# ScalarE issues the store of a tile's normed rows and the load of a later x tile, in place of SyncE

## The chip, the cores and the metric

The kernel runs on one core of a Trainium2 chip. The metric is the device time of one execution in microseconds (us). Five engines work side by side, each through its own list of instructions, in order: TensorE (PE in the profile), VectorE (DVE), ScalarE (ACT), GpSimd (POOL) and SyncE (SP), which here only issues DMAs. They meet at semaphores: an instruction can wait until a semaphore has reached a value, and can raise one when it is done.

## What is computed

The program is one layer of a Perceiver-like network on `x` (64 batches of 32 rows, 512 wide) with a context of 257 rows per batch. Cut to what matters:

```python
x = x + xattn(layernorm(x), ctx)      # 16 heads, keys = values = context, then @ W_out.T + b_out
x = x + attn(layernorm(x), ...)       # low-rank q, k, v with a rotation, 16 heads, then @ Wo + bo
x = x + ffn(layernorm(x), ...)        # 8 experts, each row to the one of its largest gate
```

The third normalisation is what the change is near. Its result is stored to a scratch tensor in DRAM, tile by tile, because the expert stage at the end gathers rows from it in another order, expert by expert:

```python
logits = xf @ Wg + bg                 # xf = layernorm(x) after the second attention
idx = argmax(softmax(logits))
out = (gelu(xf @ W1[idx] + b1[idx]) @ W2[idx] + b2[idx])
```

## The kernel before

The 2048 rows of `x` are 16 tiles of 128 rows (`T = 16`), each of four batches (`BT = 4`). Time is laid out by hand in steps: a batch has 11 steps (`STEPS`), a tile 44 (`TILE`), and every engine's program runs over the same steps and emits at each step the pieces of work that are due there. Tables of numbers (`SCALE3 = 105`, `X2 = 100`, `NORM_HI = 20` and so on) say how many steps after the start of a tile's successor a stage stands; a second table (`LATER`) shifts the last two tiles. So three tiles are in work at once: while batch b of tile t + 3 goes through the cross attention (scores, softmax, turned probabilities, product with the context), tile t + 2 goes through the dense products of the self attention (query, key and value columns, L571 to L573), and tile t is finished: its residual sum x2 is made (DVE), stored (SP, L546), measured (DVE), its root is taken (POOL), and ACT normalises it into the one buffer `norm3` (L905, from the stage `SCALE3`; the profile calls the buffer `norm`).

At that place ACT's list has, in this order: `norm_w`, the second normalisation of tile t + 2 (L905, stage `SCALE1`); `norm`, the third one of tile t (L905, `SCALE3`); `operand_hi`, the high part of tile t + 2's normed and transposed rows (L966, `NORM_HI`); then the exponentials of the next batch (L943). `operand_hi` is what DVE needs to make `operand_lo` (L1147), and PE needs both for the 48 dense products of the tile (L571 to L573), which start with a wait for `operand_lo`.

The x tiles lie in four buffers, `x_tile[t % 4]`. A buffer is free when x2 of its tile has been stored (`x2_stored`) and the third normalisation has read it (`normed_r`); then the x rows of four tiles on are loaded into it (`load_x`, L478). DVE measures them (`stats_x`, L1060, six steps later) for the first normalisation. SP's list is: the key loads of each batch (L470, four DMAs of 128 KB), the context load (L463), and in one batch of each tile the store of x2 (L546), the load of x (L478) and the store of `norm3` (L550). SP waits in order too, so what stands behind a wait waits with it.

The expert stage comes last: slots of 128 rows, gathered with indirect DMAs from both scratch tensors, with PE as the busiest engine.

Of the kernel before, what the change touches and what calls it, by code (L numbers as in the profile page):

```python
# [10 lines left out]
P = 128  # L11
# [5 lines left out]
T = B * S // P  # L17
# [30 lines left out]
SCALE3, CHOOSE, RANK, RANKED = 105, 103, 105, 106  # L48
# [130 lines left out]
def tile_at(step, offset, later=(0, 0)):  # L179

    for t in (T - 2, T - 1):
        if step == TILE * (t + 1) + offset + later[t - T + 2]:
            return t
    t, rest = divmod(step - offset, TILE)
    return t - 1 if rest == 0 and 1 <= t <= T - 2 else -1
# [15 lines left out]
def program(nc, ins, out, const_at, x2_dram, norm3_dram):  # L201
# [50 lines left out]
    x_tile = [sba(f"x_tile{i}", [P, D]) for i in range(2)] + [x_pair[:, i, :] for i in range(2)]  # L252
    norm_x, norm_w, norm3 = (sba(n, [P, D]) for n in ("norm_x", "norm_w", "norm3"))
# [98 lines left out]
    x_loaded = [signal(f"x_loaded{i}") for i in range(4)]  # L352
# [6 lines left out]
    x2_stored = [signal(f"x2_stored{i}") for i in range(4)]  # L359
    norm3_stored = signal("norm3_stored")  # L360
# [26 lines left out]
    measured_r, rstd_r, normed_r = signal("measured_r"), signal("rstd_r"), signal("normed_r")  # L387
# [66 lines left out]
    x_rows = ins["x"].rearrange("b s d -> (b s) d").rearrange("(t p) d -> t p d", p=P)  # L454


    def sync_program():
        sp, until = nc.sync, Until(nc.sync)

        def load_context(b):  # L460
            until.wait_ge(attended, 2 * (b - 4) + 2)
            src = ins["ctx_1024"][b, 0:C2 * P, :].rearrange("(p c) d -> p c d", c=C2)
            sp.dma_start(context[b % 4][:, :, :], src).then_inc(context_loaded[b % 4], 16)  # L463

        def load_keys(b):
            until.wait_ge(keys_turned, 2 * (b - 2) + 2)
            for hl in range(HL):
                src = ins["ctx_1024"][b, 0:C2 * P, hl * G * HD:(hl + 1) * G * HD].rearrange("(n j c) d -> j c n d", j=HD, c=C2)
                dst = keys[b % 2][hl * HD:(hl + 1) * HD, :, :, :, :].rearrange("p c n g d -> p c n (g d)")
                sp.dma_start(dst, src).then_inc(keys_loaded[b % 2], 16)  # L470

        def load_x(t):
            if t >= 2:
                until.wait_ge(unit_done, UNITS.index(("rot", 0)) + 1)
            if t >= 4:
                until.wait_ge(x2_stored[t % 4], 16 * (t // 4))
                until.wait_ge(normed_r, t - 3)
            sp.dma_start(x_tile[t % 4][:, :], x_rows[t]).then_inc(x_loaded[t % 4], 16)  # L478

        def load_weight(dst, name, loaded):  # L480
            sp.dma_start(dst, ins[name].rearrange("(k p) n -> p k n", p=P)).then_inc(loaded, 16)

        def broadcast(dst, name):
            src = ins[name]
            sp.dma_start(dst, src.unsqueeze(0).broadcast_to([P, src.shape[0]])).then_inc(small_loaded, 16)

        def load_small():
            broadcast(bias_xout[:, :], "L0_xattn_b_out")
            broadcast(bias_g[:, :], "L0_ffn_bg")
            sp.dma_start(out_bias[:, :], ins["L0_attn_Wo_b"].rearrange("(g p) -> p g", p=P),  # L490
                          allow_slow_non_contiguous=True).then_inc(small_loaded, 16)
            sp.dma_start(wg[:, :, :], ins["L0_ffn_Wg"].rearrange("(g p) e -> p g e", p=P)).then_inc(small_loaded, 16)
            broadcast(bias_qk[:, 0, :], "L0_attn_Wq_r_b")
            broadcast(row_uq[:, :], "L0_attn_Wu_q_b")
            broadcast(bias_qk[:, 1, :], "L0_attn_Wk_r_b")
            broadcast(row_uk[:, :], "L0_attn_Wu_k_b")
            broadcast(bias_v[:, 0:D], "L0_attn_Wu_v_b")
            broadcast(bias_out[:, :], "L0_attn_Wo_b")

        load_x(0)  # L500
        sp.dma_start(consts[:, :], ins["const"][:, 0:kept_columns]).then_inc(const_loaded, 16)
        load_keys(0)
        sp.dma_start(last_rows[0:B, :], ins["ctx_1024"][:, J - 1, :]).then_inc(last_loaded, 16)
        load_weight(staged_b[:, :, 0:DQ], "L0_attn_Wd_q_w", staged_b_loaded)
        load_weight(staged_b[:, :, DQ:2 * DQ], "L0_attn_Wd_kv_w", staged_b_loaded)
        load_keys(1)
        load_context(0)
        load_weight(staged_c[:, 2:4, :], "L0_attn_Wq_r_w", staged_c_loaded)
        load_weight(staged_c[:, 0:2, :], "L0_attn_Wu_q_w", staged_c_loaded)
        load_context(1)  # L510
        load_weight(staged_a[:, :, :], "L0_xattn_W_out", staged_a_loaded)
        load_keys(2)
        load_weight(staged_d[:, :, :], "L0_attn_Wk_r_w", staged_d_loaded)
        load_context(2)
        load_context(3)
        a, b = const_at["rope"]
        sp.dma_start(consts_1[:, :], ins["const"][:, a:b]).then_inc(tables_loaded, 16)
        a, b = const_at["before"][0], const_at["all"][1]
        sp.dma_start(tables[:, 0:b - a], ins["const"][:, a:b]).then_inc(tables_loaded, 16)

        for step in range(LAST_STEP):
            b, k = divmod(step, STEPS)
            t, bl = divmod(b, BT)
            if k == 5 and bl == 1 and t + 1 < T:
                load_x(t + 1)
            if k == 2 and 1 <= b and b + 3 < B:
                load_context(b + 3)
            if k == KEYS_LOAD_AT and 1 <= b and b + 2 < B:
                load_keys(b + 2)
            if step == UNIT_AT[4]:  # L530
                until.wait_ge(unit_done, 4)
                load_weight(staged_b[:, 0:2, :], "L0_attn_Wu_k_w", staged_b_loaded)
                load_weight(staged_b[:, 2:4, :], "L0_attn_Wu_v_w", staged_b_loaded)
            if step == BIAS_LOAD_AT:
                load_small()
            if step == UNIT_AT[13]:
                until.wait_ge(unit_done, 13)
                load_weight(staged_a[:, :, :], "L0_attn_Wo_w", staged_a_loaded)
            if step >= TILE and step % 2 == 0 and step < TILE + 2 * E:
                e = (step - TILE) // 2  # L540
                sp.dma_start(b1_all[:, E - 1 - e, :], ins["L0_ffn_b1"][e].rearrange("(k p) -> p k", p=P),
                             allow_slow_non_contiguous=True).then_inc(b1_loaded, 16)
            t = tile_at(step, X2, LATER["X2"])
            if t >= 0:
                until.wait_ge(x2_made, t + 1)
                sp.dma_start(x2_dram[t * P:(t + 1) * P, :], x_tile[t % 4][:, :]).then_inc(x2_stored[t % 4], 16)  # L546
            t = tile_at(step, SCALE3, LATER["SCALE3"])
            if t >= 0:
                until.wait_ge(normed_r, t + 1)
                sp.dma_start(norm3_dram[t * P:(t + 1) * P, :], norm3[:, :]).then_inc(norm3_stored, 16)  # L550
            if step == STEPS * (B + 1):
                until.wait_ge(attended, 2 * B)
                until.wait_ge(plast_kept, 2 * B)
                until.wait_ge(scored, 2 * B)
                until.wait_ge(k_last_moved, 2 * B)
                for e in range(EARLY):
                    load_expert(sp, e)
# [334 lines left out]
    def scalar_program():  # L892
        act, until = nc.scalar, Until(nc.scalar)
# [10 lines left out]
        def scale(x, dst, n, done):  # L904
            act.activation(dst, x, ACT.Identity, bias=shift[n][:, :], scale=rstd[n][:, :]).then_inc(done, 1)  # L905
# [40 lines left out]
        def stages(step):  # L946
            t = tile_at(step, QUERIES_MOVE)
            if t >= 1:
                place_queries(t)
            t = tile_at(step, ATT_HI, LATER["ATT_HI"])  # L950
# [4 lines left out]
            t = tile_at(step, SCALE1, LATER["SCALE1"])  # L955
# [6 lines left out]
            t = tile_at(step, NORM_HI, LATER["NORM_HI"])  # L962
# [4 lines left out]
            t = tile_at(step, Q_MOVE, LATER["Q_MOVE"])  # L967
# [32 lines left out]
            if t >= 0:  # L1000
                until.wait_ge(rstd_r, t + 1)
                until.wait_ge(norm3_stored, 16 * t)
                if t == 0:
                    until.wait_ge(bias_made, 1)
                scale(x_tile[t % 4][:, :], norm3[:, :], "r", normed_r)
            if step == PLACE_RANKS:
                until.wait_ge(in_row_made, 1)
                act.activation(row_in_row[:, 0:T - 2, :], in_row[:, 0:T - 2, :], ACT.Copy, scale=const("row")).then_inc(own_rows_made, 1)
# [11 lines left out]
        for step in range(LAST_STEP):  # L1020
# [16 lines left out]
            t = b // BT  # L1037
# [893 lines left out]
```

## Time and profile before

| what | value |
|---|---|
| three runs | 768.64, 772.24, 772.39 us; median 772.24 |
| profiled execution | 773.6 us, of which the span from first to last instruction is 771.8 |
| granted TensorE clock, mean | 0.989 |
| busy: PE, PE weight loads, DVE, ACT, POOL | 703.2, 547.1, 582.1, 430.8, 335.2 us |
| DMA, mean over the span | 167 GB/s; SP's queue 49.9% of 16 engines' span, ACT's queue 0.0% |
| one tile in the steady part | 30.7 to 32.8 us |

The busy times say which engine is nearest to its limit, over stages that differ. How much an edit costs is read from the waits at its place: an instruction that stands behind an idle stretch is released by the engine named in brackets, and only delays that reach PE's list move the end. Rows of engines are what the engine executes; rows with a "q" (SPq, ACTq) are the issue of a DMA by that engine's sequencer.

### The profile page before, as it was taken

How to read it: one execution, taken by the hardware profiler on the slowest of the kernel's cores; microseconds unless marked ns; L12 is line 12 of the kernel's file. 1: busy time of each engine (PE TensorE's matmuls, PEld its weight loads, DVE VectorE, ACT ScalarE, POOL GpSimd, SP SyncE). 2: the span in 40 equal slices, each digit the busy share in tenths (PEclk: the TensorE clock that was granted, in tenths of full speed). 3: DMA queues.
4: the chain of work that ended last, by engine and by line, in shares of the span. 5: the costliest groups of instructions: out<-in, count | busy, mean ns of one | idle time of the engine just before them, and what ended most of it. 6: DMA issues, size and time to landing. Idle time of an engine off the chain costs nothing. (4 is left out here: it accounts for less than half of the span.)

```text
span 771.8 us, 26467 instructions
## 1 busy us (share of the span) xinstructions
PE 703.2 (91%) x10598; PEld 547.1 (71%) x10598; DVE 582.1 (75%) x1185; ACT 430.8 (56%) x1081; POOL 335.2 (43%) x687
## 2 busy tenths in 40 slices
PE   5898989999999999989999899999887889999997
PEld 4546869787787787877878778788775656666664
DVE  3478678887888888888788897887565656788883
ACT  3345466675656666657566666575323545555651
POOL 1122353443434434444254443443315256866542
PEclk9999899999999999999999999999998899999999
DMA  8995445656456554564655655640604996544420
GB/s 268 303 239 110 148 136 155 166 163 157 144 158 177 154 166 148 165 184 125 171 164 162 172 148 166 172 133 23 239 16 133 376 394 237 178 151 146 141 98 5
DMA packets 114378, 129.08 MB, mean 167 GB/s; under 512 B 14478, under 2 KB 81294, under 8 KB 114256
## 3 DMA queue, kind: packets, MB, share of 16 engines
q1 hardware_dynamic: 108192, 111.12, 49.9%
q0 software_dynamic: 5520, 16.26, 6.1%
q8 instruction: 85, 1.39, 0.8%
q14 instruction: 37, 0.30, 0.1%
q10 hardware_dynamic: 544, 0.00, 0.0%
HBM read 114.77 MB, written 14.42 MB: 167 GB/s over the span
## 5 line engine op out<-in xcount | busy, mean ns | idle before, releaser
L943 ACT ACTIVATE prob<-scores,negmax 128x257 f32<-128x257 f32 x256 | 118.3, 475 | 105.0 <-DVE negmax L1143 104.9
L571 PE MATMUL stage_banks<-qkv_hi,operand_hi 128*128 128x398 f32 x256 | 97.5, 381 | 1.8 <-DVE operand_lo L1147 1.8
L1143 DVE TENSOR_REDUCE negmax<-scores 128x2 f32<-128x514 f32 x128 | 82.3, 684 | 15.0 <-PE scores L639 14.9
L572 PE MATMUL stage_banks<-qkv_lo,operand_hi 128*128 128x398 f32 x256 | 88.3, 345 | 0.1
L573 PE MATMUL stage_banks<-qkv_hi,operand_lo 128*128 128x398 f32 x256 | 88.3, 345 | 0.0
L1133 DVE STREAM_TRANSPOSE k_t<-keys 128x512 f32<-128x512 f32 x128 | 84.4, 687 | 2.6 <-DMA keys<-in_ctx 2.6
L1709 PE MATMUL stage_banks<-w_all,hidden 128*128 x184 | 82.8, 592 | 0.6 <-ACT hidden L1765 0.6
L1410 POOL COPY plast<-prob 128x2 f32<-128x2 f32 x128 | 24.6, 193 | 129.1 <-ACT prob L943 129.0
L649 PE MATMUL scores<-consts,prob 128*128 128x128 f32 x512 | 77.7, 276 | 0.3 <-ACT prob L943 0.3
L1808 DVE TENSOR_TENSOR w_lo<-w_all,w_hi 128x512 fp32r<-128x512 f32 x89 | 72.9, 877 | 0.2
L1138 DVE COPY prob_t<-scores 128x512 f32<-128x512 f32 x64 | 42.7, 668 | 30.7 <-PE scores L649 30.6
L649 PEld LDWEIGHTS scores<-consts,prob 128*128 128x128 f32 x512 | 61.5, 142 | 6.1 <-issue 1.2
L639 PE MATMUL scores<-k_t,q_t 32*32 32x257 f32 x2048 | 59.4, 394 | 6.4 <-DVE prob_t L1138 3.8
L663 PEld LDWEIGHTS att_bank<-prob_t,context 128*32 128x32 f32 x4096 | 43.3, 111 | 30.5 <-issue 30.5
L933 ACT ACTIVATE prob_t<-scores 128x512 f32<-128x512 f32 x64 | 38.4, 600 | 42.3 <-PE scores L649 41.9
L1709 PEld LDWEIGHTS stage_banks<-w_all,hidden 128*128 128x128 f32 x184 | 34.7, 189 | 35.6 <-issue 33.9
L1741 ACT ACTIVATE w_hi<-w_all 128x512 fp32r (+1 forms) x92 | 55.3, 641 | 8.3 <-PE scores L1689 5.3
L663 PE MATMUL att_bank<-prob_t,context 128*32 128x32 f32 x4096 | 50.9, 200 | 3.4 <-issue 3.3
L943 ACT ACTIVATION_READ_ACCUMULATOR prob<-scores,negmax 128x1 f32 x256 | 51.9, 203 | 0.0
L571 PEld LDWEIGHTS stage_banks<-qkv_hi,operand_hi 128*128 128x128 f32 x256 | 48.6, 190 | 3.4 <-issue 2.9
L572 PEld LDWEIGHTS stage_banks<-qkv_lo,operand_hi 128*128 128x128 f32 x256 | 48.9, 191 | 0.0
L573 PEld LDWEIGHTS stage_banks<-qkv_hi,operand_lo 128*128 128x128 f32 x256 | 48.5, 189 | 0.3 <-issue 0.3
(267 smaller groups left out, 1645.4 us busy)
## 6 DMA issues: line engine op xcount, KB each, us to landing
keys<-in_ctx SPq DMA_DIRECT2D x256, 128.0 KB, 3.2
context<-in_ctx SPq DMA_DIRECT2D x64, 512.0 KB, 4.2
w_all<-in_L_ffn_W SPq DMA_DIRECT2D x16, 1024.0 KB, 12.9
b<-in_L_ffn_b SPq DMA_DIRECT2D x23, 256.0 KB, 3.6
norm_scratch<-norm SPq DMA_DIRECT2D x16, 256.0 KB, 3.3
x_tile<-in_x SPq DMA_DIRECT2D x8, 256.0 KB, 3.7
x_pair<-in_x SPq DMA_DIRECT2D x8, 256.0 KB, 4.0
x_scratch<-x_tile SPq DMA_DIRECT2D x8, 256.0 KB, 2.2
```

What stands on the lines that cost most here:

```text
L571: pe.matmul(to, op_hi[op][:, c, :], w_hi[name][:, c, columns], start=(c == 0), stop=False)
L572: pe.matmul(to, op_hi[op][:, c, :], w_lo[name][:, c, columns], start=False, stop=False)
L573: return pe.matmul(to, op_lo[op][:, c, :], w_hi[name][:, c, columns], start=False, stop=(c == G - 1))
L639: done = pe.matmul(scores[place * S:(place + 1) * S, 2 * pair + gg, 0:J], q_t[rows, 2 * pair + gg, bl, :], k_t[pair][rows, gg, :], start=T ...
L649: done = pe.transpose(scores[:, 2 * pair, at:at + P], prob[pair][:, gg, c * P:(c + 1) * P], ident)
L663: done = pe.matmul(att_bank[place * HD:(place + 1) * HD, at:at + S], context[b % 4][:, c, h * HD:(h + 1) * HD], prob_t[pair][:, gg, c, pla ...
L943: act.activation(prob[pair][:, gg, :], scores[:, g, 0:J], ACT.Exp, bias=negmax[b % 2][:, g:g + 1], accum_out=sums[t % 2][:, g, bl:bl + 1]) ...
L1133: dve.transpose(dst, src).then_inc(keys_turned, 1)
L1143: dve.tensor_reduce(negmax[b % 2][:, 2 * pair:2 * pair + 2], scores[:, 2 * pair:2 * pair + 2, 0:J], AX.X, ALU.max, negate=True).then_inc(m ...
L1709: done = pe.matmul(bank[:, :], hidden[s % 2][:, m, :], w_of[:, bass.ds(place, 1), 1, m, :].rearrange("p a n -> p (a n)"), start=(m == 0), ...
L1741: act.activation(w1_hi[:, k, :], weights[:, k, :], ACT.Copy).then_inc(w1_cut, 1)
L1808: dve.tensor_tensor(w1_lo[:, k, :], weights[:, k, :], w1_hi[:, k, :].bitcast(F32), ALU.subtract).then_inc(w1_low, 1)
```

## The change

ACT issues two DMAs itself, right behind the third normalisation: the store of `norm3`, for which it waits on its own `normed_r`, and, while t + 4 < 16, the load of x rows t + 4, for which it waits on `x2_stored`. SP no longer issues either; it still loads the x tiles 0 to 3 and stores x2. The load of x now stands behind the store of `norm3`, where SP issued it ahead of the store.

```diff
--- before.py
+++ after.py
@@ -472,9 +472,6 @@
         def load_x(t):
             if t >= 2:
                 until.wait_ge(unit_done, UNITS.index(("rot", 0)) + 1)
-            if t >= 4:
-                until.wait_ge(x2_stored[t % 4], 16 * (t // 4))
-                until.wait_ge(normed_r, t - 3)
             sp.dma_start(x_tile[t % 4][:, :], x_rows[t]).then_inc(x_loaded[t % 4], 16)
 
         def load_weight(dst, name, loaded):
@@ -521,7 +518,7 @@
         for step in range(LAST_STEP):
             b, k = divmod(step, STEPS)
             t, bl = divmod(b, BT)
-            if k == 5 and bl == 1 and t + 1 < T:
+            if k == 5 and bl == 1 and t + 1 < 4:
                 load_x(t + 1)
             if k == 2 and 1 <= b and b + 3 < B:
                 load_context(b + 3)
@@ -544,10 +541,6 @@
             if t >= 0:
                 until.wait_ge(x2_made, t + 1)
                 sp.dma_start(x2_dram[t * P:(t + 1) * P, :], x_tile[t % 4][:, :]).then_inc(x2_stored[t % 4], 16)
-            t = tile_at(step, SCALE3, LATER["SCALE3"])
-            if t >= 0:
-                until.wait_ge(normed_r, t + 1)
-                sp.dma_start(norm3_dram[t * P:(t + 1) * P, :], norm3[:, :]).then_inc(norm3_stored, 16)
             if step == STEPS * (B + 1):
                 until.wait_ge(attended, 2 * B)
                 until.wait_ge(plast_kept, 2 * B)
@@ -1003,6 +996,11 @@
                 if t == 0:
                     until.wait_ge(bias_made, 1)
                 scale(x_tile[t % 4][:, :], norm3[:, :], "r", normed_r)
+                until.wait_ge(normed_r, t + 1)
+                act.dma_start(norm3_dram[t * P:(t + 1) * P, :], norm3[:, :]).then_inc(norm3_stored, 16)
+                if t + 4 < T:
+                    until.wait_ge(x2_stored[t % 4], 16 * (t // 4 + 1))
+                    act.dma_start(x_tile[t % 4][:, :], x_rows[t + 4]).then_inc(x_loaded[t % 4], 16)
             if step == PLACE_RANKS:
                 until.wait_ge(in_row_made, 1)
                 act.activation(row_in_row[:, 0:T - 2, :], in_row[:, 0:T - 2, :], ACT.Copy, scale=const("row")).then_inc(own_rows_made, 1)
```

ACT's list around the third normalisation of tile 0, before. `norm` is the result of the third normalisation, `norm_w` that of the second, `operand_hi` the operand of the dense products:

```order
L933 ACTIVATE prob_t<-scores 128x512 [waits attended,prob_turned]
L905 ACTIVATE norm_w<-x_pair,shift_s,rstd_s 128x512 [waits rstd_s]
L905 ACTIVATE norm<-x_tile,shift_r,rstd_r 128x512 [waits rstd_r]
L966 ACTIVATE operand_hi<-stage_banks 128x512 [waits qkv_done,norm_turned]
L943 ACTIVATE prob,sums<-scores,negmax 128x257 [waits plast_kept,maxed]
```

and the same place of the change (its lines are numbered up to 7 lower, the added ones are L1000 and L1003):

```order
L926 ACTIVATE prob_t<-scores 128x512 [waits attended,prob_turned]
L898 ACTIVATE norm_w<-x_pair,shift_s,rstd_s 128x512 [waits rstd_s]
L898 ACTIVATE norm<-x_tile,shift_r,rstd_r 128x512 [waits rstd_r]
L1000 DMA norm_scratch<-norm 128x512 [waits normed_r]
L1003 DMA x_tile<-in_x 128x512 [waits x2_stored0]
L959 ACTIVATE operand_hi<-stage_banks 128x512 [waits qkv_done,norm_turned]
L936 ACTIVATE prob,sums<-scores,negmax 128x257 [waits plast_kept,maxed]
```

Two DMAs and two waits now stand between the normalisation and `operand_hi`. So it is for tiles 0 to 11; for the last four there is the store alone.

SP's list at the same place, before:

```order
L546 DMA x_scratch<-x_tile 128x512 [waits x2_made]
L463 DMA context<-in_ctx 128x1024 [waits attended]
L478 DMA x_tile<-in_x 128x512 [waits normed_r,x2_stored0]
L550 DMA norm_scratch<-norm 128x512
L470 DMA keys<-in_ctx 32x8x128 [waits keys_turned]
L470 DMA keys<-in_ctx 32x8x128 x3
```

and of the change:

```order
L543 DMA x_scratch<-x_tile 128x512 [waits x2_made]
L463 DMA context<-in_ctx 128x1024 [waits attended]
L470 DMA keys<-in_ctx 32x8x128 [waits keys_turned]
L470 DMA keys<-in_ctx 32x8x128 x3
```

SP's key loads no longer stand behind a wait for ACT.

## Rows read from the trace of the kernel before

**Rows 1.** The page, busy time by engine (busy us, share, instructions):
```profile
PE 703.2 (91%) x10598; PEld 547.1 (71%) x10598; DVE 582.1 (75%) x1185; ACT 430.8 (56%) x1081; POOL 335.2 (43%) x687
```

**Rows 2.** Waits of PE, 130 to 540 us (waiter <- releaser: us, times, longest):
```profile
PE stage_banks L832 <- ACT soft_block L993: 14.5, 13, 1.3
PE stage_banks L571 <- DVE operand_lo L1147: 1.6, 9, 0.2
```

**Rows 3.** Timeline of PE, tile 4 (start us, us, engine line op out<-in, idle before):
```profile
270.59 0.66 PE L565 MATMUL stage_banks<-consts,norm_w 128*128 128x128 f32 x4 [0.34 <-ACT norm_w L905]
273.02 0.42 PE L571 MATMUL stage_banks<-qkv_hi,operand_hi 128*128 128x398 f32 x1 [0.17 <-DVE operand_lo L1147]
```

**Rows 4.** Timeline of ACT, tile 4:
```profile
270.44 0.80 ACT L905 ACTIVATE norm<-x_tile,shift_r,rstd_r 128x512 f32<-128x512 f32 x1
271.28 0.60 ACT L966 ACTIVATE operand_hi<-stage_banks 128x512 fp32r<-128x512 f32 x1
273.50 0.48 ACT L943 ACTIVATE prob<-scores,negmax 128x257 f32<-128x257 f32 x1 [1.62 <-DVE negmax L1143]
```

**Rows 5.** Timeline of DVE, tile 4:
```profile
269.47 1.30 DVE L1133 STREAM_TRANSPOSE k_t<-keys 128x512 f32<-128x512 f32 x2
272.11 0.16 DVE L1322 TENSOR_REDUCE rank<-logits 128x1 f32<-128x8 f32 x1
272.19 0.68 DVE L1147 TENSOR_TENSOR operand_lo<-stage_banks,operand_hi 128x512 fp32r<-128x512 f32 x1
```

**Rows 6.** Timeline of SP's queue, tile 4:
```profile
271.32 0.33 SPq L478 DMA_DIRECT2D x_tile<-in_x  x1
271.69 0.43 SPq L550 DMA_DIRECT2D norm_scratch<-norm  x1
272.17 4.00 SPq L470 DMA_DIRECT2D keys<-in_ctx  x4
```

**Rows 7.** Timeline of ACT and its queue, start of the program:
```profile
12.57 0.48 ACTq L1012 DMA_DIRECT2D low_bias<-in_L_attn_Wd_kv_b  x1
13.10 0.38 ACT L1029 ACTIVATE last_p<-stage_banks 128x256 f32<-128x256 f32 x1
```

**Rows 8.** Timeline of SP's queue, start of the program:
```profile
11.45 6.90 SPq L470 DMA_DIRECT2D keys<-in_ctx  x4
```

**Rows 9.** Timeline of SP's queue, tile 1:
```profile
176.37 1.39 SPq L550 DMA_DIRECT2D norm_scratch<-norm  x1
```

**Rows 10.** Timeline of ACT, the row normalisation of tiles 0, 1, 2, 10, 11:
```profile
144.37 0.80 ACT L905 ACTIVATE norm<-x_tile,shift_r,rstd_r 128x512 f32<-128x512 f32 x1
175.13 0.80 ACT L905 ACTIVATE norm<-x_tile,shift_r,rstd_r 128x512 f32<-128x512 f32 x1
207.02 0.80 ACT L905 ACTIVATE norm<-x_pair,shift_r,rstd_r 128x512 f32<-128x512 f32 x1
458.94 0.80 ACT L905 ACTIVATE norm<-x_pair,shift_r,rstd_r 128x512 f32<-128x512 f32 x1
491.50 0.80 ACT L905 ACTIVATE norm<-x_pair,shift_r,rstd_r 128x512 f32<-128x512 f32 x1
```

**Rows 11.** Timeline of PE, tile 1:
```profile
178.67 0.26 PE L663 MATMUL att_bank<-prob_t,context 128*32 128x32 f32 x5 [1.20 <-issue]
```

**Rows 12.** Waits of DVE, 130 to 540 us:
```profile
DVE stats_x L1060 <- DMA x_pair<-in_x: 8.1, 5, 3.3
DVE stats_x L1060 <- DMA x_tile<-in_x: 6.6, 5, 2.4
```

**Rows 13.** Timeline of DVE, tile 10:
```profile
465.88 0.69 DVE L1060 BATCH_NORM_STATS2 stats_x<-x_pair 128x6 f32<-128x512 f32 x1 [3.32 <-DMA x_pair<-in_x]
```

**Rows 14.** Timeline of ACT, tile 12:
```profile
521.63 0.81 ACT L905 ACTIVATE norm_w<-x_pair,shift_s,rstd_s 128x512 f32<-128x512 f32 x1 [0.17 <-POOL shift_s L1391]
```

**Rows 15.** The page, DMA issues (KB each, median us from issue to landing):
```profile
norm_scratch<-norm SPq DMA_DIRECT2D x16, 256.0 KB, 3.3
x_pair<-in_x SPq DMA_DIRECT2D x8, 256.0 KB, 4.0
```

## The prediction

> **What bounds the kernel now.** I read the busy shares first, then the list of waits of PE in the steady part, then the timelines of PE, ACT, DVE and SP's queue around one third normalisation. The busy shares say that PE is nearest to its limit, 91% of the span, while ACT has 56% [rows 1]. From 130 to 540 us PE's waits are few and regular, and one of them stands right at the edit: in 9 of the 12 tiles 0 to 11, PE starts the dense products (L571) with a wait for `operand_lo`, of 0.2 us at most, 1.6 us in all [rows 2]. A wait so short, and so regular, says that the chain in front of it ends together with PE's other work: there is no slack on it. The reader is to see that chain in tile 4. ACT normalises tile 4's rows from 270.44 to 271.24, starts `operand_hi` at 271.28 and ends it at 271.88 [rows 4]; DVE starts `operand_lo` at 272.19 and ends it at 272.87 [rows 5]; PE starts L571 at 273.02 after 0.17 us idle [rows 3].
>
> SP, in the same tile, issues the load of x at 271.32, so 0.08 us after the normalisation's end, and the store at 271.69 [rows 6]. Its wait for the store of x2 adds nothing to that, and it will add nothing on ACT.
>
> A delay of PE here isn't given back. Tile 1 shows it: PE loses 1.20 us there [rows 11], and the distance from its normalisation to the next is 31.89 us against 30.76 for tile 0, so 1.13 us more [rows 10]. PE's large regular wait, 14.5 us for `soft_block` [rows 2], is for ACT work that itself follows PE's scores, so it moves with PE.
>
> **What the change takes from SP.** SP's two issues (0.33 and 0.43 us, with a gap of 0.04) and the wait in front of them [rows 6]. The keys of the next batch but one could be loaded from 270.77 on, when DVE has turned the keys before them [rows 5], and SP issues them at 272.17 [rows 6]. They will go out about 1.3 us earlier. No wait of PE or DVE for keys or context from DRAM stands in the steady part, so I value this at nothing.
>
> **What it adds on ACT.** Behind the normalisation's end come the signal (0.08, as SP has it), the first issue (0.33), the gap (0.04) and the second issue (0.43), all from SP's rows [rows 6]. Does ACT go on during an issue? At the start of the program ACT's queue issues a DMA from 12.57 to 13.05, and the next ACTIVATE in its list starts at 13.10 [rows 7]: it doesn't, and takes 0.05 more. So `operand_hi` starts at 271.24 + 0.08 + 0.33 + 0.04 + 0.43 + 0.05 = 272.17 in place of 271.28, 0.89 later. DVE has a reserve: `operand_hi` ended at 271.88, its signal was there at 271.96, and `operand_lo` began at 272.19, behind DVE's own work; 0.23 of the delay are covered. It leaves 0.66 us for `operand_lo`, and for PE the same, since PE already waits. On ACT itself the time is free: 1.62 us of idle time follow `operand_hi` [rows 4], and they end at DVE's `negmax`, which stands behind `operand_lo` on DVE and moves with it.
>
> How often: the 9 tiles with that wait, and tile 11, where PE starts as late after the normalisation but the wait is too short to be listed; in tiles 1 and 6 PE is held by 1.2 us of its own and the delay is covered. 10 x 0.66 = 6.6 us. In tile 12 the normalisation comes ahead of `norm_w`, which starts 0.17 after its end [rows 14]; one issue takes 0.08 + 0.33 + 0.05 = 0.46, so 0.29 more, and PE waits for `norm_w` in every tile as in tile 4 [rows 3]: 0.3 us. In tiles 13 to 15 I take the single issues as covered, by PE's work on other parts and by ACT's waits near the end; if not, each costs up to 0.5.
>
> The bounds of the issue cost: below, 0, if ACT's next instruction ran beside the issues; above, the longest issue of such a store on SP, 1.39 us [rows 9], for both, which makes 0.08 + 2.78 + 0.09 - 0.23, so 2.7 us a tile and 27 in all. I take SP's usual rows, which are the same transfers at the same place.
>
> **The load of x.** DVE already waits for it in 10 tiles, 14.7 us together [rows 12]. How much of that reaches PE? In tile 10 DVE stands idle 3.32 us [rows 13], and the tile takes 32.56 us against 30.76 of tile 0 [rows 10]: 1.8 us reach PE, so about the first 1.5 us of such a wait are covered. The change issues the load second instead of first, 0.37 us later, behind 256 KB of store on the same queue; DVE, however, comes 0.66 later too. A store that stands second lands 3.3 us after its issue, a load that stands first 4.0 [rows 15], so the place in the queue alone needn't cost. What can cost is that 512 KB of keys are now ahead of it. The bounds: 0.37 - 0.66 = -0.3 us a tile if landing takes as long as now, and up to 1.3 (the whole lead of the keys) + 0.37 = 1.7 if it is served behind them and DVE's shift brings nothing. I take 0.3, nearer to the lower end since the load's own row moves least, for the about 7 tiles whose wait is near or above 1.5: 2 us.
>
> **Sum.** 6.6 + 0.3 + 2 = 8.9 us on the profiled execution's 773.6, so 782.5. The median of the three runs is 1.4 below the profiled one: 781.1, and I say 781. The end of the program (expert stage) gains nothing: the last store goes out at the same time, from ACT.
>
> **The rivals.**
> Rival 1, the issues themselves get long: SP now issues its four keys DMAs (4.00 us for four in tile 4, [rows 6]) at the same moment as ACT its two. If only one queue's issue is worked on at a time, each of ACT's waits for one of SP's, about 0.64 us: 1.28 more a tile, 10 x 1.28 = 12.8, so 794. Against it: at the start ACT's issue took 0.48 while SP's four keys issues took 6.90, so 1.7 each [rows 7, 8]. The Trainium skill, Perfetto Trace Analysis, section on HWDGE DMA instructions, says that the generator of descriptors is shared and locked for exclusive use, and that the wait for the lock lies inside the profiled duration. By that rule this rival would be the forecast; the 0.48 in this trace speaks against it, though a transfer of 1 KB shows little.
>
> Rival 2, the load of x lands late: its packets share the engines with the keys and the wait of DVE grows by 1.6 us. Of that about 1.3 more than I took reaches PE, in 9 tiles: 12 us, so 793. For it: the waits of 14.7 us, which show that this load is already the late one; against it: DVE's own shift. The Trainium skill, DMA: Bandwidth & Descriptors, section "Issuing engines are not separate DMA queues", says that DMAs of different issuers run on the same engines and interleave, and that a second issuer saves the sequencer's time alone. By it the own queue doesn't protect the load, and nothing is gained in transfer time.
>
> Rival 3, no change: ACT's sequencer issues beside its engine, or PE finds work in the 0.66 us. The sum is then 0.3 + 2 at most and 0 at least: 772 to 775. Against it: [rows 7], and tile 1's loss that isn't given back.
>
> Rival 4, not slower but faster, by one mechanism: the x load on a queue that has no key and context loads in front of it lands so early that DVE's wait for it goes under 1.5 us in all tiles. What the waits over 1.5 us cost PE today is 1.8 in tile 10 and less in the others, about 5 us in all. It decides from a landing 1.8 us shorter than tile 10's on. With the issues covered too it gives 767; with the 6.9 us of the issues against it, 774. Against it: the load was the first of its queue after five idle microseconds already.
>
> **How the numbers follow.** The forecast 0.57, rival 1 0.15, rival 2 0.11, rival 3 0.12, rival 4 0.05. The range is 774 to 794: below it lie rival 3's larger part and rival 4, above it the upper halves of rivals 1 and 2. A measurement of this kernel can tell about 0.5%, 3.9 us, from no change. Forecast and rivals 1 and 2 all lie above 776: slower 0.83. Rival 3 and a part of rival 4: same 0.13. Faster 0.04.
>
> **What would show it.** In the changed profile the timeline of ACT has two ACTq rows, the first about 0.08 us after each `norm`, and `operand_hi` 0.9 us after its end instead of 0.04. PE's wait before the first L571 grows from 0.17 to about 0.8 in ten tiles, and the total of L571 <- `operand_lo` from 1.6 to about 8 us. Keys go out on SP 1.3 us earlier. If ACT's issues last 0.8 to 1.4 us, rival 1 holds; if they are short and DVE's waits for x are above 25 us, rival 2; if PE's wait grows and the tiles don't get longer, the carrying through was wrong. The forecast fails if `operand_hi` starts within 0.3 us of the normalisation's end, or if DVE's waits for x vanish.

## The result, and the profile after

| | runs | median us | lowest to highest |
|---|---|---|---|
| before | 4 | 772.0 | 768.64 to 772.39 |
| the change | 4 | 791.66 | 789.53 to 793.5 |

The ratio is 1.023, with a 95% interval of 1.0186 to 1.0275: slower by 19.7 us, where 9 were forecast. A later set of runs on one chip (below, last experiment) puts it at 1.0228 (1.0198 to 1.0259). The profiled execution took 793.5 us, its span 791.7.

Nearly the whole loss lies in the stretch in which ACT issues both DMAs. From the third normalisation of tile 0 to that of tile 12 the change takes 540.39 - 144.09 = 396.30 us, in the timeline of ACT:

```profile
144.09 0.80 ACT L898 ACTIVATE norm<-x_tile,shift_r,rstd_r 128x512 f32<-128x512 f32 x1
...
540.39 0.81 ACT L898 ACTIVATE norm<-x_tile,shift_r,rstd_r 128x512 f32<-128x512 f32 x1
```

and the kernel before takes 520.65 - 144.37 = 376.28 [rows 10]:

```profile
520.65 0.81 ACT L905 ACTIVATE norm<-x_tile,shift_r,rstd_r 128x512 f32<-128x512 f32 x1
```

That is 20.0 us over twelve tiles, against a difference of the spans of 19.9. Before tile 0 ACT issues neither DMA, and from tile 12 on the stores alone; there, next to nothing is lost.

PE's waits, change, from 130 to 540 us (waiter <- releaser: us in total, times, longest), answer to [rows 2]:

```profile
PE stage_banks L825 <- ACT soft_block L986: 14.4, 13, 1.4
PE stage_banks L564 <- DVE operand_lo L1145: 9.3, 12, 0.9
PE scores L632 <- DVE prob_t L1136: 5.4, 10, 0.6
...
PE scores L632 <- DVE k_t L1131: 3.2, 5, 0.9
```

Two things grew. The wait for `operand_lo` in front of the dense products (L571 before, L564 now) went from 1.6 to 9.3 us. And PE now waits at the scores (L632) for the turned keys and for `prob_t`, both made by DVE, 8.6 us together; before, such waits came to 2.1. The wait for `soft_block`, which follows PE's own work, is as it was.

The list of waits doesn't hold the whole cost of the second. The same products also keep PE busy for longer, as their rows on the two pages show (before, then the change; after the bars: busy us and mean ns, then idle us in front of them, over the whole span):

```profile
L639 PE MATMUL scores<-k_t,q_t 32*32 32x257 f32 x2048 | 59.4, 394 | 6.4 <-DVE prob_t L1138 3.8
L632 PE MATMUL scores<-k_t,q_t 32*32 32x257 f32 x2048 | 63.6, 398 | 13.5 <-DVE prob_t L1136 8.2
```

That is 4.2 us more busy and 7.1 more idle for the same 2048 products, 11.3 together. With the 7.7 us at `operand_lo` it makes 19.0 of the 19.9.

Tile 4 shows both. ACT's timeline there, with its DMA issues (ACTq), answers to [rows 4]:

```profile
279.07 0.80 ACT L898 ACTIVATE norm<-x_tile,shift_r,rstd_r 128x512 f32<-128x512 f32 x1
279.90 0.33 ACTq L1000 DMA_DIRECT2D norm_scratch<-norm  x1
280.27 0.48 ACTq L1003 DMA_DIRECT2D x_tile<-in_x  x1
280.86 0.60 ACT L959 ACTIVATE operand_hi<-stage_banks 128x512 fp32r<-128x512 f32 x1 [0.99 <-PE stage_banks L558]
...
282.81 0.48 ACT L936 ACTIVATE prob<-scores,negmax 128x257 f32<-128x257 f32 x1 [1.36 <-DVE negmax L1141]
```

The normalisation ends at 279.87, the store is issued from 279.90, the load from 280.27 to 280.75, and `operand_hi` starts at 280.86: 0.99 us after the normalisation's end, where it was 0.04. The bracket names PE's L558, the last that `operand_hi` waits for by semaphore; but that had ended at 279.87, and what ACT did since then were the two issues. In tiles 1 and 6 the second issue took 1.47 and 1.34 us, and `operand_hi` stood 1.97 and 1.84 behind; in the same tiles SP's store issue had been as long before, 1.39 [rows 9] and 1.24. DVE, against [rows 5]:

```profile
280.73 0.16 DVE L1320 TENSOR_REDUCE rank<-logits 128x1 f32<-128x8 f32 x1
281.49 0.69 DVE L1145 TENSOR_TENSOR operand_lo<-stage_banks,operand_hi 128x512 fp32r<-128x512 f32 x1 [0.60 <-ACT operand_hi L959]
```

DVE had nothing in front of `operand_lo` any more; it waited 0.60 us for ACT. And PE, against [rows 3]:

```profile
282.33 0.42 PE L564 MATMUL stage_banks<-qkv_hi,operand_hi 128*128 128x398 f32 x1 [0.86 <-DVE operand_lo L1145]
```

0.86 us of idle time in place of 0.17. Five microseconds later the second loss comes, first on DVE, then on PE:

```profile
286.89 0.69 DVE L1058 BATCH_NORM_STATS2 stats_x<-x_tile 128x6 f32<-128x512 f32 x1 [3.51 <-DMA x_tile<-in_x]
...
287.72 1.27 DVE L1131 STREAM_TRANSPOSE k_t<-keys 128x512 f32<-128x512 f32 x2
288.92 0.65 DVE L1136 COPY prob_t<-scores 128x512 f32<-128x512 f32 x1
```

```profile
288.45 0.67 PE L632 MATMUL scores<-k_t,q_t 32*32 32x257 f32 x16 [0.61 <-DVE k_t L1131]
289.71 0.67 PE L632 MATMUL scores<-k_t,q_t 32*32 32x257 f32 x16 [0.59 <-DVE prob_t L1136]
```

DVE stood 3.51 us before `stats_x`, until the load of x had landed; the key transpositions and the copy of `prob_t` behind it were late, and PE waited 0.61 and 0.59 us for them. In the kernel before, at the same place, DVE stood 2.00 us and PE didn't wait at all:

```profile
276.07 0.69 DVE L1060 BATCH_NORM_STATS2 stats_x<-x_tile 128x6 f32<-128x512 f32 x1 [2.00 <-DMA x_tile<-in_x]
278.46 1.10 PE L639 MATMUL scores<-k_t,q_t 32*32 32x257 f32 x32
```

It also shows the longer busy time: 32 products in one go took 1.10 us, two groups of 16 with a wait between them take 0.67 each. Over the stretch DVE's waits for x went from 14.7 us in 10 tiles [rows 12] to 34.3 in 12:

```profile
DVE stats_x L1058 <- DMA x_tile<-in_x: 17.7, 6, 3.5
DVE stats_x L1058 <- DMA x_pair<-in_x: 16.6, 6, 3.8
```

because the load takes longer from issue to landing (KB each, median us), against [rows 15]:

```profile
norm_scratch<-norm ACTq DMA_DIRECT2D x16, 256.0 KB, 2.9
x_tile<-in_x ACTq DMA_DIRECT2D x6, 256.0 KB, 6.3
```

The store lands sooner than before, 2.9 against 3.3; the load, now second, takes 6.3 (6.1 for the buffers called `x_pair`) against 3.7 (4.0 for `x_pair`). SP's keys go out from 279.42, 0.45 us ahead of the normalisation's end, where they stood 0.93 behind it [rows 6]:

```profile
279.42 2.82 SPq L470 DMA_DIRECT2D keys<-in_ctx  x4
282.29 1.46 SPq L463 DMA_DIRECT2D context<-in_ctx  x1
```

PE's granted clock is 0.987 against 0.989, and plays no part.

### The profile page after: what moved, and what is told of

Read it like the earlier page. It is cut to its first block and busy times, and to the rows that moved or that the text cites. A ratio compares the mean times of both kernels' runs of the same rounds, so it can differ in the third digit from the quotient of the medians.

```text
span 791.7 us, 26455 instructions
## 1 busy us (share of the span) xinstructions
PE 707.1 (89%) x10598; PEld 546.7 (69%) x10598; DVE 583.5 (74%) x1185; ACT 430.8 (54%) x1081; POOL 335.6 (42%) x687
## 3 DMA queue, kind: packets, MB, share of 16 engines
q8 instruction: 85, 1.39, 0.7%
## 5 line engine op out<-in xcount | busy, mean ns | idle before, releaser
L564 PE MATMUL stage_banks<-qkv_hi,operand_hi 128*128 128x398 f32 x256 | 97.6, 381 | 9.6 <-DVE operand_lo L1145 9.5
L632 PE MATMUL scores<-k_t,q_t 32*32 32x257 f32 x2048 | 63.6, 398 | 13.5 <-DVE prob_t L1136 8.2
L564 PEld LDWEIGHTS stage_banks<-qkv_hi,operand_hi 128*128 128x128 f32 x256 | 48.7, 190 | 11.3 <-issue 11.0
L632 PEld LDWEIGHTS scores<-k_t,q_t 32*32 32x32 f32 x2048 | 23.5, 104 | 36.7 <-DVE k_t L1131 21.4
## 6 DMA issues: line engine op xcount, KB each, us to landing
w_all<-in_L_ffn_W SPq DMA_DIRECT2D x16, 1024.0 KB, 12.7
```

The costliest lines, as they stand in the source:

```text
L564: pe.matmul(to, op_hi[op][:, c, :], w_hi[name][:, c, columns], start=(c == 0), stop=False)
L632: done = pe.matmul(scores[place * S:(place + 1) * S, 2 * pair + gg, 0:J], q_t[rows, 2 * pair + gg, bl, :], k_t[pair][rows, gg, :], start=T ...
```

## The experiments

Each was timed beside the kernel before on the same chip; a ratio is to that, with its 95% interval.

**Two runs that each take away one reason for the late load.** The first holds SP back until `operand_hi` is made, and with it the keys and the context load that stands behind them in SP's list:

```diff
                 sp.dma_start(x2_dram[t * P:(t + 1) * P, :], x_tile[t % 4][:, :]).then_inc(x2_stored[t % 4], 16)
+            t = tile_at(step, NORM_HI)
+            if 2 <= t and t - 2 + 4 < T:
+                until.wait_ge(norm_hi, t + 1)
```

> The change, with SP held in tiles 2 to 13 until operand_hi of the tile is made, so that the keys go out behind ACT's load of x again, not ahead of it. Theory K (the load is late because 512 KB of keys now go ahead of it): the load lands in about 4.5 us in place of 6.2, DVE's waits for x fall from 34 to below 20 us, and the time falls from 791.7 to 780 to 784. Theory P (it is late because it stands second on ACT's queue, behind 256 KB of store): landing stays at about 6, waits stay above 30, time 790 to 793. Both leave PE's wait for operand_lo at about 9 us.

Measured: 1.0064 (1.0037 to 1.0092). PE's wait for `operand_lo` stays; the load lands in 4.3 us:

```profile
PE stage_banks L567 <- DVE operand_lo L1148: 8.0, 11, 0.8
```

```profile
x_tile<-in_x ACTq DMA_DIRECT2D x6, 256.0 KB, 4.3
```

DVE's waits for x are 9.7 us, less than in the kernel before. The second swaps ACT's two issues:

```diff
                 until.wait_ge(normed_r, t + 1)
-                act.dma_start(norm3_dram[t * P:(t + 1) * P, :], norm3[:, :]).then_inc(norm3_stored, 16)
                 if t + 4 < T:
                     until.wait_ge(x2_stored[t % 4], 16 * (t // 4 + 1))
                     act.dma_start(x_tile[t % 4][:, :], x_rows[t + 4]).then_inc(x_loaded[t % 4], 16)
+                act.dma_start(norm3_dram[t * P:(t + 1) * P, :], norm3[:, :]).then_inc(norm3_stored, 16)
```

> The change, with ACT issuing the load of x ahead of the store. Theory P: landing falls from 6.2 to about 4, DVE's waits for x to about 15 us, time 781 to 784. Theory K: the load goes 0.37 us earlier and lands in 5.5 or more, waits about 28, time 788 to 791. PE's wait for operand_lo stays at about 9 us in both.

Measured: 1.0111 (1.0082 to 1.0140). The load lands in 4.0 us and now the store is the late one:

```profile
norm_scratch<-norm ACTq DMA_DIRECT2D x16, 256.0 KB, 5.4
x_tile<-in_x ACTq DMA_DIRECT2D x6, 256.0 KB, 4.0
```

DVE's waits for x are 7.8 us. Each theory had said that the other's cure would not help, and both helped: the load is late only when it stands second on ACT's queue and the keys go ahead of it too. Either alone costs little. The first run came out below both theories. That both have fewer waits for x than the kernel before doesn't come from a quicker landing, which takes 3.9 to 4.3 us against 3.7 to 4.0. It comes mostly from DVE: in tile 4 it is ready for `stats_x` 3.5 us after the end of the third normalisation, where it was 2.8 before, since it is late by the first loss.

The first run doesn't separate the keys from the context load. In tile 4 of the change SP issues that load 2.4 us after the normalisation's end, before the change 5.0 us after it. No run holds one of the two alone, so where the text says that the keys go ahead, it is the keys with the context load behind them.

**The issues behind `operand_hi`.** ACT's two DMAs of tiles 0 to 11 are kept until `NORM_HI` has been emitted:

```diff
                 scale(x_tile[t % 4][:, :], norm3[:, :], "r", normed_r)
+                held.append(t)
+            if held and (held[0] + 4 >= T or tile_at(step, NORM_HI, LATER["NORM_HI"]) >= 0):
+                t = held.pop()
                 until.wait_ge(normed_r, t + 1)
```

> The change, with ACT's two DMAs of tiles 0 to 11 behind operand_hi instead of ahead of it. My theory: PE's wait for operand_lo goes back from 9.3 to about 1.6 us, which is worth 7 to 8 us, but the load goes out 0.6 us later while DVE no longer comes later, so DVE's waits for x grow by 1 us or more a tile, to 42 to 48, and 8 to 12 us of it reach PE: time 789 to 796. Rival (the delay of operand_hi is the whole loss and the waits for x are hidden): time 773 to 777.

Measured: 1.0254 (1.0188 to 1.0321), median 791.52. PE's waits:

```profile
PE scores L632 <- DVE k_t L1136: 7.7, 9, 1.2
PE scores L632 <- DVE prob_t L1141: 5.3, 9, 0.6
...
PE stage_banks L564 <- DVE operand_lo L1150: 1.6, 9, 0.2
```

The wait for `operand_lo` is gone to what it was, and nothing is won: DVE's waits for x grew to 42.4 us, and PE's for its products from 8.6 to 13.0. The time is in the range expected, but one step of the expectation is false: the load doesn't go out 0.6 us later. ACT's rows of tile 4:

```profile
278.69 0.60 ACT L961 ACTIVATE operand_hi<-stage_banks 128x512 fp32r<-128x512 f32 x1
278.70 0.33 ACTq L1005 DMA_DIRECT2D norm_scratch<-norm  x1
279.07 0.48 ACTq L1008 DMA_DIRECT2D x_tile<-in_x  x1
```

The first issue starts 0.01 us after `operand_hi` does, and the load goes out 0.41 us after the normalisation's end, as in the change (0.40). So an issue runs beside the ACTIVATE ahead of it in ACT's list, and holds up only what stands behind it. What grew is DVE's share: it is ready for `stats_x` 2.8 us after the normalisation's end instead of 3.5, and twelve times 0.7 are the 8.1 us by which its waits grew. So the loss at `operand_lo` and the loss at x aren't simply two terms to be dropped one by one: while PE and DVE are late by the first, the load has that time to land. The rival is out.

**Measuring later.** DVE's `measure` of the next x tile moves from ahead of the two key transpositions to behind them:

```diff
-MEASURE_X, ROOT_X, SCALE_X = 22, 29, 30
+MEASURE_X, ROOT_X, SCALE_X = 29, 29, 30
...
-            if k == TURN_P_AT[1] and b < B and 1 in DVE_PROB:
-                move_prob(b, 1)
             if step % TILE == MEASURE_X and t + 1 < T:
...
+            if k == TURN_P_AT[1] and b < B and 1 in DVE_PROB:
+                move_prob(b, 1)
```

> The change, with DVE's measuring of the next x tile moved behind its two key transpositions (1.3 us of work that doesn't need x). My theory (about 12 us of the loss is DVE's wait for x, over 1.5 us a tile): the waits for x fall from 34 to about 19 us, PE's waits for prob_t and k_t from 8.6 to about 1 us, time 779 to 783. Rival (the loss is all at operand_lo): time 789 to 793.

Measured: 1.013 (1.0083 to 1.0177), median 784.41, so some 7 us less than the change; the waits for x fell to 17.0 us and PE's for `prob_t` and keys to 0.2. The load still lands after 6.2 us; it only meets work that doesn't need it. The time is a little above what I had expected.

The same edit on the kernel before:

> The kernel before, with DVE's measuring of the next x tile behind its two key transpositions. My theory, that DVE's waits for x above about 1.5 us reach PE in the kernel before too (about 5 us in all): the waits fall from 14.7 to about 4 us, PE's waits for prob_t and k_t vanish, and it is 3 to 5 us faster than before, ratio 0.994 to 0.996, which would be a version better than both. Rival (later norm_x makes PE wait in its place): ratio 0.998 to 1.005, with waits of PE for norm_x of 0.5 us a tile.

Measured: 1.0045 (1.0010 to 1.0079). The waits do what I had expected, 3.5 us for x, and none of PE for `prob_t` or keys:

```profile
DVE stats_x L1060 <- DMA x_pair<-in_x: 2.9, 2, 1.7
DVE stats_x L1060 <- DMA x_tile<-in_x: 0.6, 1, 0.6
```

but the kernel isn't faster, rather 3 us slower. Nor do waits for `norm_x` appear, so it isn't the rival either. In the profile something was won: the scores' row went from 59.4 busy and 6.4 idle to 58.3 and 4.7, and from the third normalisation of tile 0 to that of tile 12 the run takes 374.41 us against 376.28. The times of the runs don't show that gain. Where it went, and the 3 us more, stays open: the profiled execution, at 771.67 us, was the shortest of its twelve.

**Three mendings at once**: issues behind `operand_hi`, load ahead of the store, measuring later (the three edits above together):

> The change with three mendings at once: ACT's two DMAs stand behind operand_hi, the load ahead of the store, and DVE measures x behind its two key transpositions. If operand_hi's delay and x's lateness are the whole loss, both go: PE's wait for operand_lo about 0 to 2 us, DVE's waits for x 4 to 10 us, time within 2 us of the kernel of before on the same chip, or 1 to 3 us below it. If there is a third cost of issuing on ACT, it shows here alone: 4 us or more above before.

Measured: 1.0022 (0.9988 to 1.0056). PE's wait for `operand_lo` is 1.6 us in 9 tiles as before, DVE's for x 8.3 us, with ACT issuing both DMAs in tiles 0 to 11:

```profile
PE stage_banks L564 <- DVE operand_lo L1150: 1.6, 9, 0.2
```

So no third cost of issuing on ACT shows; the interval's upper end leaves room for 4.3 us. Nor does a gain from SP's freed time show.

**The store alone on ACT**, the load on SP as before:

```diff
                 scale(x_tile[t % 4][:, :], norm3[:, :], "r", normed_r)
+                until.wait_ge(normed_r, t + 1)
+                act.dma_start(norm3_dram[t * P:(t + 1) * P, :], norm3[:, :]).then_inc(norm3_stored, 16)
```

(and its issue on SP taken out).

> ACT issues the store alone; SP issues the load of x as before. One issue delays operand_hi by 0.08 + 0.33 + 0.05 = 0.46 us, 0.23 of it covered: 0.2 to 0.3 us in ten tiles, so PE's wait for operand_lo is 4 to 5 us in place of 1.8, and the load lands in about 4 us. Time 2 to 4 us above before, ratio 1.003 to 1.005. If the cost were one of having ACT issue at all, rather than of the issue's length, it would be 7 us or more above.

Measured: 1.0065 (1.0031 to 1.0098), 5 us, with an interval of 2.4 to 7.6 for the 2 to 4 expected. The wait grew less than expected, to

```profile
PE stage_banks L567 <- DVE operand_lo L1145: 2.4, 9, 0.3
```

where 4 to 5 us were expected, and DVE's waits for x rose from 14.7 to 19.3: the load lands in 4.7 and 4.0 us (`x_tile`, `x_pair`) with the store beside it on ACT's queue. One issue is mostly inside DVE's reserve. Where the 5 us are, the profile doesn't say: its execution, 771.26 us, was the shortest of the ten, and from the normalisation of tile 0 to that of tile 12 it takes 376.23 us, as before.

**SP issues the store ahead of the load**, and ACT nothing:

```diff
-            if k == 5 and bl == 1 and t + 1 < T:
+            if k == 5 and bl == 1 and t + 1 < 4:
...
                 sp.dma_start(norm3_dram[t * P:(t + 1) * P, :], norm3[:, :]).then_inc(norm3_stored, 16)
+                if t + 4 < T:
+                    load_x(t + 4)
```

> The kernel before, with SP issuing the store ahead of the load. It moves the load to the second place with no keys ahead of it. If the second place alone makes it late: DVE's waits for x rise from 14.7 to 25 or more, ratio 1.007 or more. If it takes both, second place and keys ahead (as the two runs that each took one of them away suggest): it is issued 0.37 us later and lands in about 4 us, waits 18 to 20 us, ratio 1.002 to 1.005.

Measured: 1.0006 (0.9970 to 1.0042); DVE's waits for x 20.4 us, and a landing of 4.6 and 3.8. The second place alone isn't what makes the load late, as expected; the time is a little under the expected 1.002 to 1.005.

**The price of each term.** The first of the last two runs has the load ahead of the store and the later measuring, so x is in time and only `operand_hi` is delayed; the second is the change itself.

> The change with the load ahead of the store and DVE's measuring behind the two key transpositions: x is in time, operand_hi is still delayed by two issues. It prices the first term alone. My theory (each 0.7 us that PE waits for operand_lo is paid once, in about ten tiles): PE's wait for operand_lo 8 to 9 us, for x-driven k_t and prob_t near 0, time 6 to 8 us above before, ratio 1.008 to 1.011. Rival (a part of that wait is given back by PE later in the tile): ratio below 1.006.

> The change itself once more, beside the run that prices its first term, on the same chip: ratio 1.020 to 1.026. The difference between the two is what the late x costs; the sum of my two theories says 11 to 13 us, the forecast had said 2.

Measured: 1.0092 (1.0062 to 1.0122) and 1.0228 (1.0198 to 1.0259), medians 779.05 and 790.10 with 772.46 for before. PE's waits in the first:

```profile
PE stage_banks L564 <- DVE operand_lo L1145: 9.2, 12, 0.9
```

9.2 us, 7.6 more than before, for 0.0092 x 772.46 = 7.1 us of time (4.8 to 9.4 by the interval): it is paid about once. The second takes 0.0228 x 772.46 = 17.6 us, so the late x costs the other 10.5. The run with the later measuring needn't be neutral, as that edit alone gave 1.0045 on the kernel before. Two runs without it price the first term too: the load first alone (1.0111) at 8.6 us, which leaves 9.0 for the late x, and SP held back (1.0064) at 4.9, which leaves 12.7. All are far from the 2 of the forecast.

The prices hold in this order alone. With the issues behind `operand_hi`, the late x takes the whole loss: 1.0254 against 1.0022 with x in time, some 18 us, and the first term is worth nothing as long as x is late.

## Why the prediction was right in direction and short in size

**The chain at the edit: right.** That `operand_lo` has no slack, that ACT doesn't start its next instruction during an issue, and that next to nothing is given back, all came out. Predicted were 0.89 us more for `operand_hi` and 0.66 for PE; tile 4 has 0.95 and 0.69. The two issues took 0.33 and 0.48 us, where SP's rows said 0.33 and 0.43. The prediction counted ten tiles and took tiles 1 and 6 as covered by a halt of PE of its own; PE waits there too, 0.44 and 0.23 us, as the second issue is long in both. Predicted for this term: 6.9 us. Measured: 7.1 with x in time, with an interval of 4.8 to 9.4, so the closeness is in part luck.

**SP's earlier keys "at nothing": wrong, and the root of the miss.** They went out 1.4 us earlier, close to the 1.3 that I had worked out, no one waits for them, and yet they aren't free, since they and the context load behind them now share the DMA engines with the load that someone does wait for. Holding them back lets the load land in 4.3 us and gives some 12.7 us back.

**The load of x: the step that failed.** The prediction put 0.3 us a tile in about 7 tiles, 2 us, "nearer to the lower end since the load's own row moves least". The upper end of 1.7 us was nearer: DVE's waits for x grew by 19.6 us, 1.6 a tile, in all 12 tiles, and the term measured 10.5 us where 2 stood. That 1.6 is so near to 1.7 is luck. The bound had the landing grow by the keys' lead of 1.3 us and DVE's shift bring nothing; in fact the landing grew by 2.1 to 2.6 us and DVE, coming 0.7 later, took a part of it back. The reason that I gave for the low value, that the place in the queue needn't cost, is true by itself (the run with SP's store first) and false together with the keys.

**The cover of 1.5 us: about right, and not the cause of the miss.** I read it from one tile's length, which also holds what PE loses at other places. PE's own rows in that tile of the kernel before give the part of x:

```profile
467.44 0.67 PE L639 MATMUL scores<-k_t,q_t 32*32 32x257 f32 x16 [0.44 <-DVE k_t L1133]
468.70 0.67 PE L639 MATMUL scores<-k_t,q_t 32*32 32x257 f32 x16 [0.59 <-DVE prob_t L1138]
```

That is 1.0 us of waits and 0.2 by the split into two groups, for a wait of DVE of 3.32: the cover is nearer to 2 than to 1.5, and in tile 4 a wait of 2.00 cost PE nothing. Over the kernel before, the scores' row has 65.8 us busy and idle, against 62.4 with the load first and 63.0 with its own measuring later, so the waits for x cost PE some 3 us there, where I had taken 5. That the run with its measuring later isn't faster for it is open, as said.

**The rivals.** By the prediction's own sign, short issues and over 25 us of waits for x (they were 34.3), rival 2 holds. It had a chance of 0.11 and a price of 12 us on top of the 2; measured is 10.5 in all, so 8.5 on top. Rival 1, that the issues get long, is out: ACT's two took 0.33 and 0.48 us while SP was issuing its four from 279.42 to 282.24, and so in all tiles but 1 and 6. (Its 0.64 for one of SP's issues stands in no row shown: [rows 6] has 4.00 for four; where nothing holds them, SP's four take 2.55.) The Trainium skill, Perfetto Trace Analysis, section on HWDGE DMA instructions, has the descriptor generator locked for exclusive use, with the wait inside the profiled duration; at these sizes the trace shows no wait as long as one of SP's issues; a shorter one, of some hundredths, it can't rule out. Rivals 3 and 4 are out by the two intervals. The two halves had each stood in the text; the forecast took one in full and the other at the low end. The range held, its upper part being there for the rivals.

## What to carry to other kernels

A DMA issue on a compute engine costs the next instruction of that engine its full length, the signal of the result that it waits for included; here two cost 0.95 us, which matters where the next instruction feeds the busiest engine and not elsewhere. The instruction ahead of the issue in the list goes on beside it, so an issue belongs right behind the urgent instruction: there the two delayed nothing. Freeing a queue lets other transfers start earlier: ask which load someone waits for, and what will now run beside it. Put the load with a waiter ahead of the store without one: with the issues behind `operand_hi`, the load first and its reader behind other work, the same division of labour costs 0.2%, within the measurement.

## What the runs showed of the hardware

Landing of the x load, median us (the two values are those of the two buffers' names), by its place in its queue and by whether SP's keys, with the context load behind them, are issued behind it or ahead of it:

| | keys issued behind | keys issued ahead |
|---|---|---|
| load first | 3.7 and 4.0 (before, SP) | 4.0 and 3.9 (ACT) |
| load second, behind the 256 KB store | 4.6 and 3.8 (SP), 4.3 and 4.1 (ACT) | 6.3 and 6.1 (the change), 6.0 and 6.0 (its repetition) |

The SP entries hold two early loads of each buffer too. What the two queues move in tile 4 of the change, from 281 to 282 us, from 282 to 283 and from 285 to 286 (queue, kind: packets, MB, share of 16 engines; q1 is SP's, q10 ACT's):

```profile
q1 hardware_dynamic: 257, 0.12, 44.2%
q10 hardware_dynamic: 80, 0.16, 42.0%
```

```profile
q10 hardware_dynamic: 83, 0.14, 42.3%
q1 hardware_dynamic: 224, 0.11, 37.8%
```

```profile
q1 hardware_dynamic: 161, 0.19, 108.6%
q10 hardware_dynamic: 5, 0.01, 3.9%
```

At first both queues get about the same share of the engines. The Trainium skill, DMA: Bandwidth & Descriptors, section "Queues, rings and completion order", says that each DMA engine takes turns between the queues that have work; this trace agrees, with 42.0% against 44.2%. But the sharing with the keys is not the whole delay. By 284.5 us, 278 of the 288 packets of ACT's two DMAs are through; the last ten take until 286, while SP's queue, now with the 512 KB of the context load, takes about all of the engines' time (a share can exceed 100%, as packets overlap), and the load lands only behind them. In the run with the load first, it lands 4.3 us after the normalisation's end in tile 4, about when SP's queue first reaches such a share, and it is the store behind it that lands late, in 5.4 us. That the end of whatever stands second on ACT's queue meets the context load fits both runs; it is read from one tile of each, and no run moves the context load alone.
